# State products behind all output products, TensorE's waits one product sooner, and bias and statistics in other places

## What is computed

```python
x  = hidden_states                                  # (2, 512, 512)
xn = layernorm(x)
x  = x + mamba2(xn) + ffn(xn)                       # ffn: xn @ W.T + b + one chosen LoRA rank

def mamba2(h):                                      # 128 heads of 64, state 128, 8 groups, chunks of 128
    gate, hBC, dt = split(h @ in_proj_w.T)
    hs, B, C = split(silu(conv4(hBC)))
    X = hs * dt
    M = (C @ B.T per chunk) * decay(dt)             # within a chunk
    Y_diag = M @ X                                  # "chunk products"
    states = (B * decay_to_end).T @ X               # "state products", one per chunk
    S = scan over chunks(states)                    # state that enters each chunk
    Y_off = (C @ S) * exp(cumsum)                   # "off products"
    xg = (Y_diag + Y_off + D * hs) * silu(gate)
    return groupwise_rms(xg) @ out_proj_w.T         # "output products"
```

## Time and profile before

| | us |
|---|---|
| median of 3 runs | 1581.26 (1580.66 to 1581.79) |
| the profiled execution's own time | 1580.66 |
| its span, first to last instruction | 1578.9 |
| TensorE busy in the span | 1559.5 (99%) |
| VectorE, ScalarE, GpSimd busy | 1414.5, 1367.7, 1291.1 |

### The profile page before, as it was taken

How to read it: one execution, slowest core, us unless ns; L and a number is a source line. 1 busy time by engine, 2 the same in 40 slices (tenths; PEclk the granted TensorE clock), 3 DMA queues, 4 the chain that set the end, 5 groups by cost and what they waited for, 6 DMA issues and landing times.

```text
span 1578.9 us, 29209 instructions
## 1 busy us (share of the span) xinstructions
PE 1559.5 (99%) x9172; PEld 1271.9 (81%) x9172; DVE 1414.5 (90%) x2343; ACT 1367.7 (87%) x2620; POOL 1291.1 (82%) x1614
## 2 busy tenths in 40 slices
PE   8999999999999999999999999999999999999998
PEld 7877888888888888887778788888888888888886
DVE  6988999999999999999979898898898888888887
ACT  4678899999999999989846899999999999999996
POOL 5549998999999998989874488778787878787786
PEclk9999999999999999999999999999999999999999
DMA  5257767676776676766614666766667667667673
GB/s 178 94 171 223 197 214 221 196 226 195 220 225 198 213 224 199 220 202 208 198 42 142 201 198 222 218 201 225 212 200 230 200 210 222 199 221 215 202 225 92
DMA packets 231754, 311.83 MB, mean 197 GB/s; under 512 B 144176, under 2 KB 160560, under 8 KB 231344
## 3 DMA queue, kind: packets, MB, share of 16 engines
q1 hardware_dynamic: 231600, 309.97, 63.9%
HBM read 240.69 MB, written 36.70 MB: 176 GB/s over the span
## 4 chain that ended last, share of the span: by engine, by line
PE 87%; DVE 5%; POOL 4%; issue 2%; ACT 1%; DMA 1%; SPq 0%; DVEq 0%; ACTq 0%; POOLq 0%
PE bg L804 21%; PE bo L975 20%; PE bt L804 12%; PE bh L804 11%; PE by L1031 7%; PE bg L1053 7%; PE bt L1018 3%; PE bh L1018 2%; PE bo L783 1%; POOL wl L631 1%; DVE cv L1085 1%; PE bo L862 1%; POOL xl L734 1%; DMA turned<-tg 1%; POOL wol L750 1%
## 5 line engine op out<-in xcount | busy, mean ns | idle before, releaser
L407 ACT ACTIVATE mt<-cs_row,cs_tok 128x128 f32<-128x128 f32 x1024 | 324.5, 390 | 0.0
L631 POOL TENSOR_TENSOR wl<-raw,wh 128x256 fp32r<-128x256 f32 x328 | 250.2, 792 | 59.1 <-ACT wh L379 59.1
L725 POOL COPY xt<-turned 128x512 uint16<-128x512 uint16 x248 | 202.3, 862 | 42.3 <-DMA turned<-tg 42.3
L716 POOL TENSOR_TENSOR mt<-mt,gt 128x256 f32<-128x256 f32 x128 | 118.0, 943 | 141.7 <-ACT mt L588 141.2
L741 POOL TENSOR_TENSOR sqa<-sqa,sq 128x256 f32<-128x256 f32 x222 | 223.7, 1027 | 1.0 <-ACT sq L561 1.0
L750 POOL TENSOR_TENSOR wol<-raw_o,woh 128x256 fp32r<-128x256 f32 x256 | 190.4, 764 | 10.5 <-ACT woh L528 10.5
L734 POOL TENSOR_TENSOR xl<-xg,xh 128x256 fp32r<-128x256 f32 x254 | 189.7, 768 | 6.0 <-ACT xh L541 6.0
L1085 DVE SCALAR_TENSOR_TENSOR cv<-bt,par_sb,cv 128x511 f32<-128x511 f32 (+2 forms) x192 | 143.7, 748 | 49.3 <-ACT cv L383 44.8
L1085 DVE SCALAR_TENSOR_TENSOR cv<-bh,par_sb,cv 128x511 f32<-128x511 f32 (+2 forms) x192 | 143.7, 748 | 35.4 <-ACT cv L383 30.9
L379 ACT ACTIVATE wh<-raw 128x1024 fp32r<-128x1024 f32 (+1 forms) x146 | 152.3, 1043 | 0.7 <-DMA raw<-in_w_dtag 0.7
L975 PE MATMUL bo<-woh,xl 128*128 128x512 f32 x508 | 149.1, 415 | 0.4 <-POOL xl L734 0.4
(11 more groups left out here) (215 smaller groups left out, 3814.7 us busy)
## 6 DMA issues: line engine op xcount, KB each, us to landing
raw<-in_w_step SPq DMA_DIRECT2D x128, 512.0 KB, 4.6
cs_row<-cs_rows SPq DMA_DIRECT2D x128, 512.0 KB, 7.0
low_parts<-wl SPq DMA_DIRECT2D x64, 512.0 KB, 5.8
raw_o<-in_w_out SPq DMA_DIRECT2D x128, 256.0 KB, 5.7
wl<-low_parts SPq DMA_DIRECT2D x64, 512.0 KB, 4.7
ec_row<-ec_rows SPq DMA_DIRECT2D x256, 96.0 KB, 5.7
raw<-in_w_bc SPq DMA_DIRECT2D x16, 512.0 KB, 3.6
acc<-in_x SPq DMA_DIRECT2D x8, 256.0 KB, 5.4
```

What stands on the lines that cost most here:

```text
L407: e = act.activation(mt[:, m % 2, h, chunk(j)], cs_row[:, m % 2, h, chunk(j)], ACT.Relu, bias=cs_tok[:, j, 2 * m + h:2 * m + h + 1], scale ...
L631: e = pool.tensor_tensor(wl[:, n % 2, cols], raw[:, n % 2, cols], wh[:, n % 2, cols].bitcast(F32), ALU.subtract)
L725: e = pool.tensor_copy(to[:, half], turned[:, NJ * half:NJ * (half + 1), :])
```

## The change

On TensorE, in the 124 steps with `early_state`, set 2 of the output products now comes right after set 1, and the state products right after it, directly in front of the chunk products. The waits of each small group are moved into the group ahead of it, in front of its last product: those of the state products in front of the last output product, those of the chunk products in front of the last state product, those of the off products (and of `sum_squares`) in front of the last chunk product, and the next step's wait for weights in front of the last off product. What is waited for is the same, except that the off products' wait now has `v_s` count 2 in it from the start (the second off product had it), and the second off product waits for count 4 (the third had it). On GpSimd, `add_bias` moves from steps 2 to 5 into the prologue, behind the weight splits of `g` = 4 to 7. On VectorE, statistics and normalization stand ahead of the convolution taps (line 1085) of the same step instead of ahead of the updates of `S`.

```diff
@@ GpSimd
                 if j == 0:
                     pool.wait_ge(ld_wb, 48)
+                    pool.wait_ge(p_lo, b + 1)
                     pool.wait_ge(pv, b * PRO_DVE + PRO_DVE_LORA)
@@
                     if g == 3:
                         add_ffn(b)
+                    if g >= GROUPS - NJ:
+                        add_bias(b, g - (GROUPS - NJ))
@@
-                    if 2 <= m < 2 + NJ:
-                        add_bias(b, m - 2)
@@ TensorE
+                    def await_states():
+                        pe.wait_ge(v_xd, did(n - 1))
...
+                    def await_chunks():
+                        pe.wait_ge(v_x, did(n - 1))
+                        pe.wait_ge(v_m, did(n - 1))
...
+                    def await_off():
+                        pe.wait_ge(v_sg, did(min(n, b * STEPS + STEPS - 1)))
+                        pe.wait_ge(v_off, did(n - 2))
+                        pe.wait_ge(a_s1, did(n - 1))
+                        pe.wait_ge(v_s, did(n - 1, 4, 2))
@@ output
                                 for j in range(NJ):
+                                    if then and k == ks[-1] and j == NJ - 1:
+                                        then()
@@
-                            output(range(2) if early_state else range(3))
+                            output(range(3), await_states if early_state else None)
@@
                         for c in range(NS):
+                            if early_state and c == NS - 1:
+                                await_chunks()
                             mm = pe.matmul(other[:, chunk(c)], btok[:, g, c, :], xd[:, c, :], start=True, stop=True)
                         mm.then_inc(t_st, 1)
-                        if early_state:
-                            output((2,))
@@
                         for j in range(NJ):
                             for h in range(2):
+                                if early_state and j == NJ - 1 and h == 1:
+                                    if ends:
+                                        await_squares()
+                                    await_off()
                                 mm = pe.matmul(yb[HD * h:HD * (h + 1), chunk(j)], xt[:, j, HD * h:HD * (h + 1)],
@@
                         for c in range(NS):
-                            if c == 0:
-                                pe.wait_ge(a_s1, did(n - 1))
-                            else:
-                                pe.wait_ge(v_s, did(n - 1, 4, 2 * c))
+                            if c == 1:
+                                pe.wait_ge(v_s, did(n - 1, 4, 4))
+                            if c == NS - 1 and early_state and has(m + 1):
+                                await_weights(b, step(b, m + 1))
@@ VectorE
+                    if b + 1 < NB and STEPS - 12 <= m < STEPS - 6:
+                        h, part_of = divmod(m - (STEPS - 12), 3)
+                        if part_of < 2:
+                            stats_of(b + 1, 2 * h + part_of)
+                        else:
+                            variance(b + 1, h)
+                    if b + 1 < NB and STEPS - NJ <= m < STEPS:
+                        norm(b + 1, m - (STEPS - NJ))
                     if has(m):
                         for k in range(1, TAPS):
                             tap(n, un, u, mine, k)
...
-                    if b + 1 < NB and STEPS - 12 <= m < STEPS - 6:
...
-                        norm(b + 1, m - (STEPS - NJ))
                     if has(m - 1):
                         dve.wait_ge(a_s1, did(n - 1))
```

More of the change, by code:

```diff
@@ L791, in tokens, with await_weights, project @@
                 return lambda k: t[:, b, k, :] if j is None else t[:, b, k, chunk(j)]
-            def project(dst, b, n, kind):
+            def await_weights(b, n):
                 pe.wait_ge(a_wh, did(n))
+            def project(dst, b, n, kind, awaited=False):
+                if not awaited:
+                    await_weights(b, n)
                 for i, (w, t) in enumerate(((wh, xTh), (wh, xTl), (wl, xTh))):
@@ L934, in sum_squares, with await_squares, output @@
                         return mm
-                    def output(ks=range(3)):
+                    def await_states():
+                        pe.wait_ge(v_xd, did(n - 1))
+                        if not by_dma(b, m - 1):
+                            pe.wait_ge(v_x, did(n - 1))
+                        if m > 2 and (m - 2) % PER_GROUP == 0:
+                            pe.wait_ge(v_ms, did((n - 2) // PER_GROUP - 1))
+                        if m == 1:
+                            pe.wait_ge(a_bt, did(b * GROUPS + (GROUPS - 1)))
+                    def await_chunks():
+                        pe.wait_ge(v_x, did(n - 1))
+                        pe.wait_ge(v_m, did(n - 1))
+                        if b + 1 == NB:
+                            pe.wait_ge(p_m, m)
+                        if bank_y(b, m - 1) is by:
+                            pe.wait_ge(v_xg, did(n - 2))
+                    def await_squares():
+                        pe.wait_ge(v_h2, did(un))
+                        pe.wait_ge(p_sqa, squares(b, m - 2))
+                    def await_off():
[3 more added lines that the diff above has]
+                        pe.wait_ge(v_s, did(n - 1, 4, 2))
+                    def output(ks=range(3), then=None, awaited=False):
                         first, very_last = (m - 2) % PER_GROUP == 0, n - 2 == NB * STEPS - 1
@@ L970, in output @@
                                 a, c = parts[k]
-                                wait_low(k)
+                                if not awaited:
+                                    wait_low(k)
                                 for j in range(NJ):
+                                    if then and k == ks[-1] and j == NJ - 1:
+                                        then()
                                     if k == 0:
@@ L982, in _ @@
                             pe.wait_ge(v_h2, did(un - 4 + m))
-                        project(mine, b, step(b, m), 0).then_inc(t_hs, 1)
+                        project(mine, b, step(b, m), 0, awaited=m > 2).then_inc(t_hs, 1)
                         if m == 0:
@@ L1009, in _ @@
                         g = (m - 1) % GROUPS
[L1010 to L1016, removed]
+                        if not early_state:
+                            await_states()
                         for c in range(NS):
+                            if early_state and c == NS - 1:
+                                await_chunks()
                             mm = pe.matmul(other[:, chunk(c)], btok[:, g, c, :], xd[:, c, :], start=True, stop=True)
                         mm.then_inc(t_st, 1)
-                        if early_state:
-                            output((2,))
                         yb = bank_y(b, m - 1)
[L1023 to L1028, removed]
+                        if not early_state:
+                            await_chunks()
                         for j in range(NJ):
                             for h in range(2):
+                                if early_state and j == NJ - 1 and h == 1:
+                                    if ends:
+                                        await_squares()
+                                    await_off()
                                 mm = pe.matmul(yb[HD * h:HD * (h + 1), chunk(j)], xt[:, j, HD * h:HD * (h + 1)],
@@ L1045, in _ @@
                     if has(m - 1):
-                        pe.wait_ge(v_sg, did(min(n, b * STEPS + STEPS - 1)))
-                        pe.wait_ge(v_off, did(n - 2))
+                        if not early_state:
+                            await_off()
                         for c in range(NS):
-                            if c == 0:
-                                pe.wait_ge(a_s1, did(n - 1))
-                            else:
-                                pe.wait_ge(v_s, did(n - 1, 4, 2 * c))
+                            if c == 1:
+                                pe.wait_ge(v_s, did(n - 1, 4, 4))
+                            if c == NS - 1 and early_state and has(m + 1):
+                                await_weights(b, step(b, m + 1))
                             mm = pe.matmul(bg[:, chunk(c)], S[:, c, :], ct[:, g, chunk(c + 1)], start=True, stop=True)
```

2 lines of the change are left out of this document (removed).

## The result

| | before | changed |
|---|---|---|
| median, us | 1581.21 (5 runs, 1580.66 to 1581.79) | 1617.69 (5 runs, 1617.46 to 1620.0) |
| profiled execution, us | 1580.66 | 1617.46 |
| span, us | 1578.9 | 1615.7 |

The ratio is 1.0234, with a 95% interval of 1.0219 to 1.0249: slower by 36.5 us. The forecast was 1609, range 1594 to 1626.

A forecast was written before the change was run, and what follows sets the result against it. TensorE, busy 99% of the span, was taken to bound the kernel. A loss of 34.7 us from the unmet wait, less 2.1 (bias) and 3.9 (statistics), gives +28.7 on 1580.66: 1609 us, range 1594 to 1626.

The forecast's parts named there:

- The order alone: TensorE's new product order without any wait: chunk products start at T0 + 1.67 instead of T0 + 1.69, gaining 0.02 a step.
- The chain: From T0, the old state products' start: ScalarE copies the state at T0 + 1.78, VectorE updates `S` from T0 + 2.08.
- The load: Last chunk product waits for `S[:, 1]`, loading at T0 + 2.60 instead of 2.27; off products start 0.25 later than before.
- the added waits: Three signals beyond its own that the last chunk product waits for: 0.03 a step allowed, bounds nothing and 0.15.
- Rival 1: Even met waits cause the load gaps at TensorE's width changes; both gaps go, steps stay equal, moves give 1574.7 us; 6%.
- Rival 2: `S[:, 1]` is there by T0 + 2.27, 0.33 sooner than counted, so TensorE does not stop: 1572 us; 2%.
- Rival 3: TensorE's stop costs more: 0.15 for extra waits, 0.40 a step, 1624 us; with queue refill up to 1640; above 1626, 9%.
- Rival 4: Last chunk product restarts faster: 0.20 a step, 1599 us, or 0.16, 1594; inside the forecast range, within its 80%.
- Bias: GpSimd's bias pieces leave steps 2 to 5, where they make `xd` late: gain 2.1 us.
- Statistics: VectorE's statistics ahead of the taps no longer lengthen eleven steps: gain 3.9 us, bounds 2 and 3.9.
- Sum: Whole kernel: 34.7 lost, less 2.1 and 3.9 gained, is +28.7 us on 1580.66.
- the main term: TensorE's stop for `S[:, 1]` ahead of the last chunk product: 0.28 x 124 = 34.7 us lost.

The follow-up runs named there:

- the waits at home: The changed kernel with every wait of TensorE back at its old place, keeping the new product order and the bias and statistics moves: 1580.85 us, ratio 1.0001.

## Why the prediction was right

- **The order alone.** Forecast -0.02 a step; 0.03 in the steady step with the waits at home. But over the kernel it was worth nothing (1580.85 against 1580.82), for the waits for `xl` in 25 loads. I had put "perhaps 15 of the steps, so 2 us at most", and then nothing, because the longer step covers them; in the changed kernel that held, as a statement on the order it was too small.
- **The chain.** Forecast copy T0 + 1.78, updates T0 + 2.08; measured 1.77 and 2.09. Each link came from a row of a step in which it was not hindered, and the sum held.
- **The load.** Forecast T0 + 2.60 and 0.03 for the added waits; measured 2.67. From there 0.36 to the off load; measured 0.37. So the step grew by 0.32 and not 0.28: 39.7 us and not 34.7. The mis-sized term is the price of the added waits: 0.03 in the forecast, 0.06 or so measured, for a late signal in an instruction of its own.
- **Rival 1, the waits are the gaps.** Out: the 0.17 ahead of the off products is there with the waits at home (21.5 us in 123 loads), with all sooner (22.6, where the first off product has no wait of its own), and however many chunk products stood behind the stop. The gap goes with the change of width, as by the rule that the prediction takes from the Trainium skill, TensorEngine Tiling (Array Packing), Key Properties; that it is a drain of the engine, no run shows.
- **Rival 2, the chain in time.** Out by the 14 and 2 loads. **Rival 3** (0.40 a step) overstated the stop; its further term, a queue to be refilled, up to 1640, came from no row, and no run shows such a term. **Rival 4** (0.20) understated the stop.
- **Bias.** Forecast -2.1; in the changed kernel 4 x 11.10 exactly, alone -2.0.
- **Statistics.** Forecast -3.9 with bounds 2 and 3.9; -0.3 in the changed kernel, and no gain on TensorE's old program either. This step failed. I looked for what is queued behind the statistics on VectorE and whether it has slack, and not for what the normalization itself waits for at its new place: `rstd`. The miss, 3.6 us, is outside the bounds that I gave this term.
- **Sum.** Both errors went the same way, +5.0 and +3.6: 28.7 became 37.3, and 36.8 was measured. The range was wide enough for both. The mechanism of the main term was right, and its size came out within 5 us.

## What to carry to other kernels

A wait moved ahead by one small product costs nothing if its signal has come, and stops everything behind it if not. Before moving it, count the unhindered chain to the signal from rows, and compare with the start of the instruction that will now carry it; if a stop is left, put the late signal on the instruction itself and the met ones in front. Two moves that are each sound take each other's cover: here the output products that left the space between state and chunk products were what kept `S` in time. And a moved piece of work must be asked two things: who stands behind it, and what does it itself wait for at the new place.

## What was not expected of the hardware

- A late signal costs TensorE 0.06 us more when it is waited for in a separate instruction ahead of the load than on the load itself (0.95 against 0.89 from the start of `S` to the off load; 5.8 us over 124 steps).
- Two products of 64 columns each, on different halves of the array, cost after a stop hardly more than one: 0.40 against 0.37 to the next load.
- The gap at the change of width ahead of the off products, 0.17 of load idle, was the same wherever the waits stood, as the prediction counted on, and also where TensorE had just stopped, which no row of the kernel before could show.
